# Layers 0 and 3 of a four-layer convolution and attention network: every load of patches and taps to 128 partitions, base rows and planes in DRAM by half of the array, row and channel

## What is computed

```python
# layer 0
base = _conv1x1(x, w_qkv)                       # 192 -> 576 channels
qkv = concatenate([_dwconv(base, w_dw3, 1), _dwconv(base, w_dw5, 2), _dwconv(base, w_dw7, 3)], axis=1)
qkv = _conv1x1(qkv, w_pconv)                    # 1728 -> 576
...                                             # attention over channels, three top-k softmaxes, projection
# layer 1: attention over channels; layer 2: a selective scan
# layer 3
w: (192, 1, 7, 7), b: (192,)                    # depthwise 7 x 7 with bias
```

## Time and profile before

| | us |
|---|---|
| runs | 2520.53 median of 3 (2518.78 to 2528.45) |
| the profiled execution | 2517.25 |
| its span | 2515.5 |
| PE busy in the span | 1945.1 (77%) |
| DVE busy | 1287.4 (51%) |
| POOL busy | 870.2 (35%) |
| ACT busy | 804.7 (32%) |
| HBM read, written | 299.33 MB, 121.96 MB |
| mean granted clock of PE | 0.883 of 2.4 GHz |

### The profile page before, as it was taken

The page is one execution under the profiler, slowest core; times in us unless marked ns, Lnnn a source line. Parts: engine busy times, 40 slices in busy tenths (PEclk is TensorE's granted clock), DMA queues, the critical chain, the costliest instruction groups (busy, mean ns, idle before and its releaser), DMA issues. The chain is left out here.

```text
span 2515.5 us, 36893 instructions
## 1 busy us (share of the span) xinstructions
PE 1945.1 (77%) x15660; PEld 1203.3 (48%) x15660; DVE 1287.4 (51%) x1313; ACT 804.7 (32%) x1269; POOL 870.2 (35%) x459
## 2 busy tenths in 40 slices
PE   3879779769999999999978768777777777774052
PEld 1577666667777777777734322222222222221031
DVE  6445444441111111111271166799999999988803
ACT  3445445440000000000122125633543533335410
POOL 3334233220000000000000040599899899983300
PEclk9889899889999999999988778899899979987555
DMA  7899999988131313130120040678688868863799
GB/s 197 249 311 314 316 292 304 296 257 241 59 118 59 118 60 118 60 118 1 43 59 11 0 139 21 156 197 219 171 213 216 209 175 213 218 179 90 224 215 294
DMA packets 195538, 424.51 MB, mean 169 GB/s; under 512 B 18733, under 2 KB 143661, under 8 KB 184717
## 3 DMA queue, kind: packets, MB, share of 16 engines
q1 hardware_dynamic: 182540, 414.81, 58.8%
q10 hardware_dynamic: 12832, 7.34, 1.1%
HBM read 299.33 MB, written 121.96 MB: 167 GB/s over the span
## 5 line engine op out<-in xcount | busy, mean ns | idle before, releaser
L743 PE MATMUL ps<-mem 128*128 128x288 f16 x5376 | 654.6, 287 | 14.4 <-DMA mem<-depthwise_out 14.4
L743 PEld LDWEIGHTS ps<-mem 128*128 128x128 f16 x5376 | 502.1, 98 | 152.9 <-issue 15.4
L1717 POOL TENSOR_TENSOR mem<-mem 128x1024 f32<-128x1024 f32 x192 | 465.7, 2444 | 45.3 <-ACT mem L1651 42.9
L1626 PE MATMUL ps<-mem 128*128 128x512 f32 x768 | 417.9, 676 | 39.1 <-POOL mem L1717 35.0
L1112 POOL TENSOR_TENSOR mem<-mem 128x1536 f16<-128x1536 f32 x16 | 50.8, 3180 | 940.3 <-ACT mem L1090 940.3
L533 PE MATMUL ps<-mem 56*96 56x240 f16 (+1 forms) x5184 | 308.2, 280 | 86.1 <-DMA mem<-base_phases 53.0
L533 PEld LDWEIGHTS ps<-mem 56*96 56x96 f16 x5184 | 297.7, 128 | 111.4 <-DMA mem<-base_phases 58.5
L786 DVE TENSOR_TENSOR mem<-ps,mem 128x128 f16<-128x128 f32 x64 | 18.7, 292 | 586.8 <-ACT mem L807 586.8
L1746 DVE TENSOR_TENSOR_SCAN mem<-mem,ps 128x1024 f32<-128x1024 f32 x132 | 307.8, 2332 | 18.2 <-issue 10.3
L646 DVE TENSOR_TENSOR mem<-ps,mem 96x1024 f16<-96x1024 f32 x144 | 175.3, 1220 | 217.9 <-ACT mem L578 217.9
L1626 PEld LDWEIGHTS ps<-mem 128*128 128x128 f32 x768 | 153.5, 213 | 242.9 <-issue 134.5
(11 more groups left out here) (202 smaller groups left out, 1915.4 us busy)
## 6 DMA issues: line engine op xcount, KB each, us to landing
mem<-l_bc SPq DMA_DIRECT2D x504, 256.0 KB, 4.5
depthwise_out<-mem SPq DMA_DIRECT2D x105, 512.0 KB, 9.4
mem<-depthwise_out SPq DMA_DIRECT2D x31, 1664.0 KB, 10.8
mem<-base_phases SPq DMA_DIRECT2D x72, 448.0 KB
base_phases<-mem SPq DMA_DIRECT2D x56, 512.0 KB, 9.9
mem<-in_wd SPq DMA_DIRECT2D x72, 336.0 KB
mem<-l_planes SPq DMA_DIRECT2D x48, 252.0 KB
mem<-in_x SPq DMA_DIRECT2D x4, 2048.0 KB, 13.6
```

Of the source, the lines that this page charges most:

```text
L743: ins = nc.tensor.matmul(ps[:, 2 * (i % 2) + h, 0:HALF], d, pw[rows, wa, k, HALF * h:HALF * h + HALF], start=(k == 0 and n == 0), stop=(k ...
L1626: ins = nc.tensor.matmul(py[:, a, :], ident, hh[:, n % 4, 512 * a:512 * a + 512], start=(n % N == 0), stop=(n % N == N - 1))
L1717: nc.gpsimd.tensor_tensor(hh[:, n % 4, :], hh[:, n % 4, :], cs[:, n % 4, :], ALU.mult).then_inc(hc_pool, 1)
```

## The change

Windows and taps of both layers come to all 128 partitions in one DMA each: the arrays in DRAM get 64 rows for each half of PE's array instead of 56, and rows 56 to 63 are zeros. PE still contracts over 56 rows.

- `base_phases` becomes [2 halves, 64 rows, 288 channels, 512]. The channels of a tile are reordered in the weights (`wbase`), so that one half lies on the first partitions of the tile and the other on the rest. Each store of base or shifted rows becomes two, from half of the partitions each. A window load is one DMA of 128 x 8192 bytes.
- The taps `wd` are [128, ...], one DMA of 128 x 6144 bytes a batch instead of two of 56.
- `l3_planes` becomes [2 halves, 64 rows, 96 channels, 2 images, 288]. A window load is one DMA of 128 x 9216 bytes in a row instead of four with runs of 576 bytes. The stores of planes are now the ones with runs of 576 bytes, two for each old one, from half of its partitions, one issued by SP and one by ACT.
- The unused rows of both arrays are stored once, from cleared memory, in the first block of layer 0: six DMAs of 96 x 8 x 1024 bytes, and two of 96 x 8 x 1152. POOL clears `ext` first for this, and its first shift waits for these stores.
- x is also given as `x_rows` [128, 3, 4096], the layout on chip, and loaded with four DMAs of 128 partitions, all by SP.
- Layer 3: the low parts of the taps go from POOL to DVE. The second tile's planes are stored before the third tile is normalised; the first three windows are loaded before the third tile's planes are stored; the sums of a batch go out in four DMAs instead of two.

```diff
@@ group_norm
-                    sp.dma_start(xt[:, t, :], x_dram[t, 0:128, :]).then_inc(loaded[t], 16)
+                    sp.dma_start(xt[:, t, :], x_dram[:, t]).then_inc(loaded[t], 16)
-                    sp.dma_start(xt[0:64, 2, s], x_dram[0, 128:192, s]).then_inc(rest_loaded[h], 16)
+                    sp.dma_start(xt[:, 2, s], x_dram[:, 2, s]).then_inc(rest_loaded[h], 16)
...
-                    act.dma_start(xt[64:128, 2, s], x_dram[1, 128:192, s]).then_inc(rest_loaded[h], 16)
@@ layer0_depthwise
     def load_taps(sp, n):
-        for t in range(2):
-            sp.dma_start(w32[n % NTB][64 * t:64 * t + TAPROWS], inp["wd"][TAPROWS * t:TAPROWS * (t + 1), n * BP * TAPS0:(n + 1) * BP * TAPS0]
-                         ).then_inc(w_loaded[n % NTB], 16)
+        sp.dma_start(w32[n % NTB], inp["wd"][:, n * BP * TAPS0:(n + 1) * BP * TAPS0]).then_inc(w_loaded[n % NTB], 16)
+    def store_unused(sp, t):
+        size = B * 2 * PLANE
+        src = ext[0:C // 2].rearrange("c s r n -> c (s r n)")[:, 0:(64 - TAPROWS) * size].rearrange("c (r n) -> c r n", n=size)
+        sp.dma_start(planes_d[t, TAPROWS:64].rearrange("r c b n -> c r (b n)"), src).then_inc(sem.unused_planes, 16)
...
+        sp.wait_ge(ext_cleared, 1)
+        for t in range(2):
+            for k in range(3):
+                sp.dma_start(base_d[t, TAPROWS:64, 96 * k:96 * k + 96].rearrange("r c n -> c r n"),
+                             ext[0:96, 0:2].rearrange("c a r n -> c (a r) n")).then_inc(rest_stored, 16)
+            store_unused(sp, t)
...
-                sp.dma_start(base_d[4 * g:4 * g + 4, 128 * m:128 * m + width(m)].rearrange("r c n -> c r n"),
-                             stb[0:width(m), j % NSTB]).then_inc(base_stored[j % NSTB], 16)
+                for t in range(2):
+                    sp.dma_start(base_rows(m, t, 4 * g), half(stb[:, j % NSTB], m, t)).then_inc(base_stored[j % NSTB], 16)
...
-                for t in range(2):
-                    sp.dma_start(win[64 * t:64 * t + TAPROWS, slot], base_d[:, c0 + BP * t:c0 + BP * t + BP]).then_inc(win_loaded[slot], 16)
+                src = base_d.rearrange("t r c n -> (t r) c n")[:, BP * n:BP * n + BP]
+                sp.dma_start(win[:, n % NWIN], src).then_inc(win_loaded[n % NWIN], 16)
...
             split_taps(0)
-            pool.wait_ge(ext_cleared, 1)
+            pool.wait_ge(rest_stored, 96)
+            pool.wait_ge(sem.unused_planes, 32)
@@ layer3
+    def store_planes(eng, t, h):
+        for p0, b, c0, n in pieces(t):
+            lo = p0 + n // 2 * h
+            eng.dma_start(planes_d[h, 0:TAPROWS, c0 // 2:c0 // 2 + n // 2, b].rearrange("f c n -> c f n"),
+                          pl[lo:lo + n // 2, t % 2].rearrange("p c r h n -> p (c r) (h n)")).then_inc(stored[t], 16)
...
+            def load_windows(n):
+                src = planes_d.rearrange("t f c b n -> (t f) c (b n)")[:, BP * n:BP * n + BP]
+                sp.dma_start(win[:, n % NW], src).then_inc(win_in[n % NW], 16)
+            for t in range(2):
                 sp.wait_ge(rows_done, t + 1)
+                store_planes(sp, t, 0)
+                sp.wait_ge(tap_hi, t + 1)
+                sp.wait_ge(tap_lo, t + 1)
+                load_taps(sp, t + 2)
...
+            sp.wait_ge(stored[1], used + 32)
+            for n in range(NW):
+                load_windows(n)
+            sp.wait_ge(rows_done, NT)
+            store_planes(sp, 2, 0)
+            for n in range(NW, NB3):
+                sp.wait_ge(conv_sum, n - NW + 1)
                 if CB * n == 128:
-                    sp.wait_ge(stored[2], used + 32)
+                    sp.wait_ge(stored[2], used + 64)
+                load_windows(n)
...
+                if t == 2:
+                    taps(3)
...
                 rows(t)
+                for i in ((0,), (1, 2), ())[t]:
+                    taps(i)
```

More of the change, by code:

```diff
@@ L282, in _ @@
         def _(act):
-            if x_dram is not None:
-                for h in range(2):
-                    s = slice(HW // 2 * h, HW // 2 * (h + 1))
-                    act.dma_start(xt[64:128, 2, s], x_dram[1, 128:192, s]).then_inc(rest_loaded[h], 16)
             act.wait_ge(ready, L + 1)
@@ L428, in _, with base_rows, half @@
         def _(sp):
+            def base_rows(m, t, row):
+                return base_d[t, row:row + 4, 64 * m:64 * m + width(m) // 2].rearrange("r c n -> c r n")
+            def half(v, m, t):
+                return v[width(m) // 2 * t:width(m) // 2 * (t + 1)]
             def store_base(m, g):
@@ L1880, in _ @@
                 sp.wait_ge(rows_done, t + 1)
-                for p0, b, c0, n in pieces(t):
-                    sp.dma_start(planes_d[b, c0:c0 + n].rearrange("c f n -> c (f n)"),
-                                 pl[p0:p0 + n, t % 2].rearrange("p c r h n -> p (c r h n)")).then_inc(stored[t], 16)
+                store_planes(sp, t, 0)
+                sp.wait_ge(tap_hi, t + 1)
+                sp.wait_ge(tap_lo, t + 1)
+                load_taps(sp, t + 2)
             sp.wait_ge(tap_hi, NPIECE)
@@ L1885, in _ @@
             sp.wait_ge(tap_lo, NPIECE)
[L1886 to L1897 removed]
+            sp.wait_ge(sem.unused_planes, 32)
@@ L1900, in _ @@
-            sp.wait_ge(stored[2], used + 32)
+                sp.wait_ge(conv_stored[k], 64 * (128 // CB // NSTG))
+            sp.wait_ge(stored[2], used + 64)
             for t in range(NT):
@@ L1952, in shift_right, with store_second @@
                 nc.scalar.copy(grid(pl[:, k, 8:11])[:, :, :, 1:8], grid(pl[:, k, 5:8])[:, :, :, 0:7]).then_inc(shifted, 1)
+            def store_second(t):
+                act.wait_ge(rows_done, t + 1)
+                store_planes(act, t, 1)
             normalise(0)
             taps(0)
-            for t in range(NT):
-                shift_right(t)
-                if t + 1 < NT:
-                    normalise(t + 1)
-                taps(t + 1)
+            shift_right(0)
+            normalise(1)
+            store_second(0)
+            taps(1)
+            shift_right(1)
+            taps(2)
+            store_second(1)
+            normalise(2)
+            taps(3)
+            shift_right(2)
+            store_second(2)
             for n in range(NB3):
@@ L1967, in _ @@
                 for b in range(B):
-                    dst = conv_d[b, CB * n:CB * n + CB].rearrange("(g j) (f n) -> (j f) g n", j=4, f=M3)
-                    act.dma_start(dst, stg[:, n % NSTG, :].rearrange("p (g b n) -> p g b n", g=4, b=B)[:, :, b]).then_inc(conv_stored[n % NSTG], 16)
-        @block.gpsimd
-        def _(pool):
-            def taps(i):
-                pool.wait_ge(tap_hi, i + 1)
-                s = slice(3 * WC * i, 3 * WC * (i + 1))
-                q = slice(0, 64 + TAPROWS)
-                nc.gpsimd.tensor_tensor(wh[q, 1, s], w32[i % 2][q], wh[q, 0, s], ALU.subtract).then_inc(tap_lo, 1)
-            for i in range(NPIECE):
-                taps(i)
+                    for t in range(2):
+                        dst = channels(conv_d, b, n)[t].rearrange("(h j) (f n) -> (j f) h n", j=4, f=M3)
+                        src = stg[:, n % NSTG, :].rearrange("p (t h b n) -> p t h b n", t=2, h=2, b=B)[:, t, :, b]
+                        act.dma_start(dst, src).then_inc(conv_stored[n % NSTG], 16)
         @block.vector
@@ L1998, in rows, with taps @@
                 ins.then_inc(rows_done, 1)
+            def taps(i):
+                dve.wait_ge(tap_hi, i + 1)
+                s, q = slice(3 * WC * i, 3 * WC * (i + 1)), slice(0, 64 + TAPROWS)
+                V.tensor_tensor(wh[q, 1, s], w32[i % 2][q], wh[q, 0, s], ALU.subtract).then_inc(tap_lo, 1)
             for k in range(2):
@@ L2005, in _ @@
                 if t == 2:
-                    dve.wait_ge(stored[0], used + 16)
+                    dve.wait_ge(stored[0], used + 32)
                 for r in range(4):
@@ L2046, in layouts @@
     wq = v["L0_conv_w_qkv"].T
-    o["wbase"] = np.stack(packed_rows(wq), 1)
+    tiles = [np.arange(m, min(m + 128, QKV)).reshape(-1, 2, BP).transpose(1, 0, 2).reshape(-1) for m in range(0, QKV, 128)]
+    o["wbase"] = np.stack(packed_rows(wq[:, np.concatenate(tiles)]), 1)
     dws = [v["L0_conv_w_dw3"][:, 0], v["L0_conv_w_dw5"][:, 0], v["L0_conv_w_dw7"][:, 0]]
-    wd = np.zeros((2, TAPROWS, QKV // 2, TAPS0), f)
+    wd = np.zeros((2, 64, QKV // 2, TAPS0), f)
     place = {(1, q, ro): 32 * q + 8 * ro for q in range(3) for ro in range(4)}
```

82 lines of the change are left out of this document (36 added, 46 removed).

## The result

The change made the kernel faster: 2497.2 us (median of 7, 2491.05 to 2512.59) against 2520.76 (median of 7), a ratio of 0.9914 (95% interval 0.9896 to 0.9931), some 22 us. The forecast was 63. The direction and the range held; the size did not. All three terms of the sum came out smaller than forecast: layer 0's stage gave about nothing for 27, layer 3 gave 18 for 30, and the start cost 6 where it should have given 6.

The account below looks back on a forecast made before the run. The prediction took DMA to bound layer 0's depthwise stage and layer 3's windows. Its terms, -27 - 6 - 30 = -63 us, took the profiled 2517.25 to 2454, predicted as a median of 2457 us; range 2405 to 2500.

Parts of the forecast that it names:

- Layer 0's stage: Layer 0's depthwise stage: each period of eight batches 6 us shorter, over 4.5 periods -27 us (bounds -81 to +71).
- wide loads: Layer 0's depthwise stage: two loads a batch on 128 partitions instead of four on 56, taken as -9 us a period.
- stores in halves: Layer 0's base rows: 140 stores from half as many partitions instead of 70, 0 to +10 us a period, taken as +3.
- PE could follow: Layer 0's depthwise stage: without its waits and the slowed batches, PE needs 85 us a period.
- 4.7 more: Layer 0's period: three batches take 9.3 to 9.4 us where one took 7.74, 4.7 us more.
- B: Rival: layer 0's loads no faster, engines carrying the same number of rows; stage 0, start -4, layer 3 -25: 2491 us; chance 0.20.
- C: Rival: half-partition stores of base rows and planes run as when alone, base rows +10 us a period; 2584 us; chance 0.07.
- A: Rival: layer 0's stage reaches its lower bound, -81, with -9 at the start and -42 in layer 3: about 2388 us; chance 0.10.
- The start: Layer 0's beginning: x arrives sooner, statistics done at 23 to 26 us against 32.6; -6 us (-9 to +3).
- Layer 3 before the windows: Layer 3's beginning: DVE freed of 17 us of collisions, tap splits 11 us, first windows issued at 2368 to 2376 us.
- Layer 3's windows: Layer 3: windows 40 us, tile 2's planes 18, sums 17, together 75, end at 2446; taken as -30 us.
- D: Rival: layer 3's last tap load sits behind plane stores until 2390, windows gain only 5 us: 2482 us; chance 0.08.

Follow-up runs that it names:

- early_taps: Changed kernel with ACT splitting the next batch's high taps after the batch's first unit instead of its second: 2477.14 us, 0.9828 of the kernel before.
- narrow_early: Changed kernel with taps split one unit earlier and layer 0's window and tap loads each as two DMAs of 56 partitions: 2502.28 us, 0.9932 of before.
- zero_src: Changed kernel with unused rows stored from zeros in DRAM in four DMAs of long runs, POOL not waiting for them: 2489.68 us, 0.9884 of before.
- again: The changed kernel run again without any edit, for a second profile: 2501.16 us, 0.9931 of the kernel before.
- interleave: Changed kernel with tile 2's four plane stores all on SP, one ahead of each of windows 3 to 6: 2497.48 us, 0.9912 of before.
- l3_only: Kernel before with only the new layer 3 and its taps, plus stores of the planes' unused rows in layer 0's first block: 2505.6 us, 0.9936 of before.

## Why the prediction was right and wrong

**Layer 0's stage, forecast -27: the step that failed.** The stage took 467.2 and 479.6 us where it was 471.0 before: about nothing was won. The prices of its parts were both too large, and their errors partly cancelled: wide loads, forecast -9 a period or -40 in 4.5, measured -21; stores in halves, forecast +3 a period or +13, measured about +2. Their sum was forecast as -27 and is -19 in the stage with the chain out of the way (443.9 against 463.4); that this is so near is luck. What failed is the sentence that "PE could follow: without its waits and the slowed batches it needs 85 us". It took the 2.79 us wait for POOL out together with the waits for windows, as if it were part of DMA's backlog. It is a bound of its own, with an end that no load moves, and it is mostly followed by matmuls at the lower clock level: the prediction had counted exactly those as "4.7 more". When the windows came sooner, more batches reached it, and two met DVE's split of weights (waits for POOL 21.3 to 43.9 us; PE busy 308.2 to 323.4). early_taps shows it: 24 us from one line, 9 in the kernel before. How much of the 24 is the meeting with DVE, some 5 us each time, was not tried by itself.

**Rivals for this stage.** B (0 for the stage, 2491) has nearly the measured time, but not its mechanism: wide loads are faster, by 21 us in the stage (narrow_early). By the rule on DMA engines that the prediction named (the Trainium skill, DMA: Bandwidth & Descriptors, Why a DMA increments its semaphore by 16 and not by 1) the term would have been 0. narrow_early measured otherwise, and that decides; no run here shows how many engines a load used, but its packets were shorter (455 and 360 ns), which a count of rows leaves out. C falls as well: stores from 64 partitions in the mix cost about 2 us in the stage, not 10 a period, though planes stored alone do run at 231 against 398. The Trainium skill states that 64 adjacent partitions reach half of the ports (SBUF — State Buffer, Door 1: The DMA port swizzle): the planes stored alone agree with it, and in the mix no such cost shows. A falls: the stage never came to its lower bound.

**The start, forecast -6, measured +6 (profiles).** x came as forecast; the statistics ended at 22.6. The step that failed is the one on the unused rows: they were charged to DMA ("19 us at 337") and to POOL's shift, which "can catch up"; but SP itself is held while it issues them, and the block's end waits for SP, so every engine waits. zero_src shows it: 12.7 us sooner with the same bytes in long runs (taken against the 42.90 of the first profile; 13.7 against `again`, 43.90). A term at nothing was the second block, 2.7 us longer in the changed kernel and 2.8 in zero_src (46.6); why stays open.

**Layer 3 before the windows, forecast first sum 20 us sooner: right**, 21.5. No copy of a border column takes DVE over 0.7 us where one took 4.79 (the shifted planes, 2688 elements a row, take 1.16), the splits of taps took 2.55 for the 2.8 estimated. The first window was issued 63.6 us after the layer's start, where 66.1 was measured before: 2.5 us sooner, 3 forecast. The tap loads did sit behind planes, as in D (SP 5.23 and 9.37 in their issue, ACT waits 7.14 and 5.55 for them), but not until 2390.

**Layer 3's windows, forecast 75 us from the first windows to the last sum, measured 91.8** (2373.16 to 2464.95). The step that failed is the sum of 75 us, 24.6 MB in three terms that each run at their own rate, or 328 GB/s together. DMA moved 27.96 MB from 2373 to 2465, at 304 GB/s and a share of 0.94. The 24.6 MB at 304 are 81 us, 6 more than forecast; the other 3.4 MB, 11 us, are the loads that bring the sums back, issued from 2450.54 on, before the last sum is out, for which the forecast had taken off 5. This is an account by bytes; no run has the loads of the sums later. The low rate shows best at "the planes of tile 2 ... 18 us at 231": their four stores with runs of 576 bytes stand between windows 2 and 3 and ahead of ACT's sums on the same DMA engines: from 2386 to 2406 DMA moves 204 GB/s at a share of 0.87, the next stretch 361, PE waits 11.85, and the first two sums take 14.24 and 12.06 to issue, where 1.9 was taken. The steps between sums were 79.3 / 11 = 7.2 us, not 5 to 6. Where these stores stand seems the smaller part: in its profile interleave won some 4 us. So the layer gave -18 instead of -30; l3_only says 16.

Together, in `again` against the profile before: the start +6.4, the stage -3.8, layer 3 -18.4, 15.8 of the 16.7 us between the two spans, where -6, -27 and -30 were forecast. The 2497.2 us lie in the range of 2405 to 2500, 3 us from its end, and the range reached that far because it took in B and D, whose mechanisms are not what happened: that it held is luck. Why one profile of the changed kernel has more slow batches than the other stays open, as does what leaving the unused rows unstored would give, which wasn't tried.

## What to carry to other kernels

Before a resource is made faster, list every other wait in the same rhythm with what it hangs on, also the short ones and the ones that are hidden now, and ask of each whether it moves when the bottleneck does: here a wait of 2.78 us, with the slow matmuls behind it, took all that faster loads won, and moving one line gave it back. Price a DMA by its issue too, on the queue that issues it, where many short runs go out ahead of a barrier. A padding that makes transfers whole has to be written once, and how it is written (128 long runs from DRAM or thousands of short ones from on-chip memory) can decide the sign of the start.

## What the runs showed of the hardware

- The issue of DMAs with many short runs, behind other traffic, lasted long: three stores of 96 x 8 runs of 1024 bytes held SP for 15.88 us; one store of 128 long runs with the same 2.36 MB, out of DRAM instead of on-chip memory, held it for 2.72. Sums with short runs held ACT for up to 14.70 us behind planes.
- Stores from 64 partitions instead of 128, in a mix with other traffic, cost too little to see, 465.3 us against 463.4, though planes stored alone from 64 partitions run at 231 GB/s against 398.
- Packets of one load from 128 partitions were shorter than those of two loads from 56: 360 against 455 ns on average for 8192 bytes, 306 against 357 for 6144, in the same mix.
- Three subtracts of POOL that take 1.92 us together took 6.7 to 7.3 beside a DVE subtract of 4.34 us with two on-chip inputs, in all twelve cases, in eight profiles, where they had begun 1.5 to 1.6 us before DVE's. Before, DVE's copies took longer beside POOL.
- A wait of 2.78 us was followed by some 5 us of matmuls at the lower clock level, in eight of nine cases in the changed kernel but in two of five in the one before (42 of 55 and 2 of 10 over all profiles with that order of taps): the wait then costs about as much again behind it, and when it does was not settled.
